# One transposition and one correction product per pair, bias rows per label, and a first pair that mixes time halves as they arrive

## What is computed

```python
x = x + conv_ssm(x masked to t < length[b])       # per channel: causal convolution, kernel of 1024 taps
x = x + einsum('bct,bcd->bdt', x, mix[cond[b]])   # 64x64 matrix of one of 16 conditions, over channels
x = x + x @ W2.T + bias2 + (x @ A2[a[b]].T) @ B2[a[b]].T      # T x T, LoRA of rank 16, 32 adapters
x = x + x @ W3.T + 0.5 * (x @ A3[l[b]]) @ B3.T                # T x T, LoRA of rank 32, 5 labels
```

## Time and profile before

| | |
|---|---|
| median of 3 runs | 1446.25 us (1444.93 to 1446.51) |
| profiled execution, its own time | 1442.18 us |
| span of the core in it | 1440.4 us |
| granted TensorE clock, mean | 1.0 |
| TensorE busy | 1429.8 us, 99% |
| VectorE / ScalarE / GpSimdE busy | 78% / 43% / 7% |
| preparation, convolution, dense part begin at | 0, 177, 549 us |

### The profile page before, as it was taken

The page is one execution under the profiler, slowest core; times in us unless marked ns, Lnnn a source line. Parts: engine busy times, 40 slices in busy tenths (PEclk is TensorE's granted clock), DMA queues, the critical chain, the costliest instruction groups (busy, mean ns, idle before and its releaser), DMA issues.

```text
span 1440.4 us, 31629 instructions
## 1 busy us (share of the span) xinstructions
PE 1429.8 (99%) x9368; PEld 1329.8 (92%) x9368; DVE 1127.4 (78%) x2288; ACT 612.7 (43%) x1217; POOL 100.9 (7%) x193
## 2 busy tenths in 40 slices
PE   9999999999999999999999999999999999999998
PEld 7888899999999999999999999999999999999997
DVE  7975498888888887777777777787777777778775
ACT  4331376666666663333433433433343343343331
POOL 2322100000000002000000000000000000000000
PEclk9999999999999999999999999999999999999999
DMA  8033288888888886564564565556556556555652
GB/s 315 1 129 79 76 283 272 276 277 272 277 268 276 273 274 183 170 203 148 166 200 146 162 197 163 153 182 190 153 162 204 146 161 203 153 153 190 182 154 81
DMA packets 117070, 271.94 MB, mean 189 GB/s; under 512 B 24173, under 2 KB 60401, under 8 KB 114381
## 3 DMA queue, kind: packets, MB, share of 16 engines
q1 hardware_dynamic: 107048, 237.86, 54.1%
q10 hardware_dynamic: 9990, 33.68, 5.8%
HBM read 198.59 MB, written 72.85 MB: 188 GB/s over the span
## 4 chain that ended last, share of the span: by engine, by line
PE 95%; DVE 2%; DMA 2%; SPq 0%; issue 0%; POOL 0%; ACT 0%; DVEq 0%; POOLq 0%; ACTq 0%
PE ps L796 18%; PE ps L789 17%; PE ps L1704 14%; PE ps L788 12%; PE ps L769 8%; PE ps L1603 7%; PE ps L1715 6%; PE ps L805 4%; PE ps L1695 3%; PE ps L1707 2%; PE ps L1589 1%; PE ps L780 1%; PE ps L1612 1%; DMA p<-in_L_cond_base_weight 1%; DMA out<-y_out 1%; PE ps L775 1%
## 5 line engine op out<-in xcount | busy, mean ns | idle before, releaser
L789 PE MATMUL ps<-weights,xa 128*128 128x352 f32 x1152 | 323.0, 322 | 0.0
L788 PE MATMUL ps<-weights,xa 128*128 128x256 f32 x1152 | 321.8, 281 | 0.5 <-ACT y_out L597 0.5
L796 PE MATMUL ps<-weights,xs 128*128 128x512 f32 x1152 | 291.2, 401 | 0.0
L796 PEld LDWEIGHTS ps<-weights,xs 128*128 128x128 f32 x1152 | 207.0, 189 | 40.4
L1704 PE MATMUL ps<-toep,ut 128*128 128x512 f32 (+2 forms) x1152 | 226.7, 342 | 0.0
L788 PEld LDWEIGHTS ps<-weights,xa 128*128 128x128 f32 x1152 | 217.3, 189 | 2.5 <-issue 1.1
L789 PEld LDWEIGHTS ps<-weights,xa 128*128 128x128 f32 x1152 | 216.2, 188 | 1.3
L1704 PEld LDWEIGHTS ps<-toep,ut 128*128 128x128 f32 x1152 | 194.3, 189 | 16.6
L568 ACT ACTIVATE a<-ps 128x512 f32<-128x512 f32 x128 | 76.7, 599 | 281.9 <-PE ps L769 281.2
L769 PE MATMUL ps<-m_gath,x_in 128*128 128x128 f32 x1024 | 134.6, 275 | 1.3 <-DVE x_in L660 1.3
L769 PEld LDWEIGHTS ps<-m_gath,x_in 128*128 128x128 f32 x1024 | 126.6, 191 | 4.0 <-DVE x_in L660 1.5
(11 more groups left out here) (227 smaller groups left out, 2255.3 us busy)
## 6 DMA issues: line engine op xcount, KB each, us to landing
xt<-in_xt SPq DMA_DIRECT2D x64, 512.0 KB, 5.7
x_d<-yo SPq DMA_DIRECT2D x64, 512.0 KB, 2.9
x_nat<-in_x SPq DMA_DIRECT2D x64, 512.0 KB, 3.8
lags<-kern_d SPq DMA_DIRECT2D x63, 512.0 KB, 5.0
x_in<-x_d SPq DMA_DIRECT2D x62, 512.0 KB
out<-y_out ACTq DMA_DIRECT2D x62, 512.0 KB, 5.8
stack<-b_d SPq DMA_DIRECT2D x130, 128.0 KB, 3.9
tab<-a_d SPq DMA_DIRECT2D x128, 128.0 KB, 2.1
```

What stands on the lines that cost most here:

```text
L788: mm(acc[:, left, 0:HALF], x_part, w[:, 0:HALF], start=start, stop=end, skip_group_check=True)
L789: ins = mm(acc[:, right, 0:HALF + KR], x_part, w[:, HALF:WIDE], start=start, stop=end, skip_group_check=True)
L796: ins = mm(acc[:, bank], operand[:, a, i, :], plain(i, b, m), start=opens and i == a == b == 0, stop=i == K4 - 1 and a == 1, skip_group_ch ...
```

## The change

- **Pair, TensorE.** One `hrow`, `hc` and `c_gath` of 128 rows holds both tiles (64 rows each), so one `turn(n)` and one `adapters(n)` serve the pair. `turn` stands in the middle of M6, `adapters` after `quarter(n + 1, 1)`; M4 is no longer cut in two. `low_rank(0, 0, PIECES_S)`, which stood before `quarter(n + 1, 1)`, stands after M3, immediately before `quarter(n + 1, 2)`. Tile 1 has its high rows at 64 and its low rows at 0.
- **Pair, VectorE.** One `h_columns` instead of two, and both `h_stack` after the addition that sets `u2_read`. `first_low(n+1)` comes before `h_columns`.
- **Pair, ScalarE.** No line of it is in the diff.
- **Bias rows.** `row_d` holds a row pair (high and low) for each of the 5 labels. `load_stack` loads two bias rows per batch element, `load_c` no longer loads a bias row. Per pair SyncE issues 12 loads for the stacks (8 before) and 4 for the correction matrix (8 before). `pair_ids` reads four numbers at once; there are four such calls per pair in place of twelve single reads.
- **Preparation.** Bias times A3 moves from job `c` to job `a3b`; job `c` gets five products of one column that turn that row; job `row` gets two more products. `b3n` is loaded and scaled earlier.
- **Start of the dense part.** The last channel's rows go in two halves of time, the front half as soon as it is there. The first pair chooses and mixes three quarters, runs M1, and mixes the fourth after it. The low part of tile 1's table follows the first two choices. `keep_clock` runs 6 products. GpSimdE fills fewer and larger tiles.

```diff
+    b3n, _ = at("b3n", [P, T], F32, o_c - AR // P * 4 * T)
...
-    EVEN_ROWS, LANDED_FIRST = C - 4, 16 * 6
+    EVEN_ROWS, LANDED_FIRST = C - 4, 16 * 4
...
-    FILL_START, FILL_BETWEEN = 20, 12
+    FILL_START, FILL_BETWEEN = 20, 6
...
+    def pair_ids(n, base_of):
+
+        limit = A2N if base_of == B else L3N
+        _, values = nc.values_load_multi_w_load_instructions(index[0:1, bass.ds(4 * n + base_of, 4)], engines=[mybir.EngineType.SP],
+                                                             min_val=0, max_val=limit - 1)
+        return values[0:2], values[2:4]
 
...
+    last_halves = [[sem(f"last_half{h}_{v}") for v in range(2)] for h in range(2)]
+
+    def last_rows(eng, c, v, landed, cols=slice(0, T)):
 
         for b in range(2):
             row = b * C + c
-            eng.dma_start(x1_in[v][row:row + 1], yo[c % 2][2 * v + b:2 * v + b + 1]).then_inc(landed, 16)
-
-    masked = sem("masked")
-
-    def load_stack(eng, v, a):
+            eng.dma_start(x1_in[v][row:row + 1, cols], yo[c % 2][2 * v + b:2 * v + b + 1, cols]).then_inc(landed, 16)
+
+    masked, stack_cleared = sem("masked"), sem("stack_cleared")
+
+    HIGH, LOW = (0, KS), (KS, 0)
+
+    def load_stack(eng, v, a, l):
 
         for b in range(2):
             row = b * (R2 + R3)
-            eng.dma_start(f(stack[v][row:row + R2]), b2_d[bass.ds(a[b], 1)].squeeze(0)).then_inc(stack_landed[v], 16)
-            eng.dma_start(f(stack[v][KS + row:KS + row + R2, 0]),
-                          b2_d[bass.ds(a[b], 1), :, 0, :].squeeze(0)).then_inc(stack_landed[v], 16)
+            high, low, bias = HIGH[v] + row, LOW[v] + row, LOW[v] + 2 * b
+            eng.dma_start(f(stack[v][high:high + R2]), b2_d[bass.ds(a[b], 1)].squeeze(0)).then_inc(stack_landed[v], 16)
+            eng.dma_start(f(stack[v][low:low + R2, 0]), b2_d[bass.ds(a[b], 1), :, 0, :].squeeze(0)).then_inc(stack_landed[v], 16)
+            eng.dma_start(f(stack[v][bias:bias + 2, 1]), row_d[bass.ds(l[b], 1)].squeeze(0)).then_inc(stack_landed[v], 16)
...
-                rows = slice(b * (R2 + R3), b * (R2 + R3) + R2)
-                cols = bass.ds(l[b] * R3, R3)
-                sp.dma_start(c_gath[v][rows, H3], c_adapters[bass.ds(a[b], 1), :, cols].squeeze(0)).then_inc(c_landed[v], 16)
-                sp.dma_start(c_gath[v][KS + b:KS + b + 1, H3], c_d[AR:AR + 1, cols]).then_inc(c_landed[v], 16)
+                row = v * KS + b * (R2 + R3)
+                to = c_gath[row:row + R2, v * KS + R2:v * KS + R2 + R3]
+                sp.dma_start(to, c_adapters[bass.ds(a[b], 1), :, bass.ds(l[b] * R3, R3)].squeeze(0)).then_inc(c_landed[v], 16)
...
+                sp.wait_ge(stack_cleared, 1)
                 for v in range(2):
-                    load_stack(sp, v, first_ids[v])
+                    load_stack(sp, v, first_ids[v], first_ids[2 + v])
                 return
+            a, l = pair_ids(n, B), pair_ids(n, 2 * B)
             sp.wait_ge(p_done, n)
             for v in range(2):
-                load_stack(sp, v, ids(sp, n, v, B))
+                load_stack(sp, v, a[v], l[v])
...
-            a, l = [ids(sp, n + 1, v, B) for v in range(2)], [ids(sp, n + 1, v, 2 * B) for v in range(2)]
+            a, l = pair_ids(n + 1, B), pair_ids(n + 1, 2 * B)
             for v in range(2):
                 sp.wait_ge(h_lo[v], n + 1)
                 load_tables(sp, v, a[v], l[v])
-            sp.wait_ge(adapted, 2 * n + 2)
+            sp.wait_ge(adapted, n + 1)
...
+            pool.wait_ge(last_halves[0][v], 32)
+            pool.wait_ge(last_halves[1][v], 32)
+        nc.gpsimd.tensor_copy(c_gath[:], ident[:]).then_inc(c_fixed, 1)
+        nc.gpsimd.memset(f(stack[1][0:KS, 1]), 0.0).then_inc(stack_cleared, 1)
+        nc.gpsimd.memset(hrow[:], 0.0).then_inc(small_fixed, 1)
+        nc.gpsimd.memset(f(hs[1][0:KS, 1]), 0.0).then_inc(small_fixed, 1)
+        pool.wait_ge(small_fixed, 2)
...
+                nc.gpsimd.tensor_tensor(hs[v][rows, 1, b * C:(b + 1) * C], pair_of[0], pair_of[1], ALU.add).then_inc(small_fixed, 1)
...
-        def h_columns(n, v):
-            dve.wait_ge(turned, 2 * n + v + 1)
-            nc.vector.tensor_copy(hc[v][0:KS], acc[0:KS, SMALL_BANK, 0:P]).then_inc(hc_ready, 1)
+        def h_columns(n):
+            dve.wait_ge(turned, n + 1)
+            nc.vector.tensor_copy(hc[:], acc[:, SMALL_BANK, 0:P]).then_inc(hc_ready, 1)
 
         def h_stack(n, v):
-            low = acc[0:KS, SMALL_BANK, P:2 * P]
-            dve.wait_ge(adapted, 2 * n + v + 1)
-            nc.vector.tensor_copy(hs[v][0:KS], low.unsqueeze(1).to_broadcast([KS, 2, P])).then_inc(hs_hi, 1)
+            high, low = slice(HIGH[v], HIGH[v] + KS), slice(LOW[v], LOW[v] + KS)
+            of = acc[high, SMALL_BANK, P:2 * P]
+            dve.wait_ge(adapted, n + 1)
+            nc.vector.tensor_copy(hs[v][high], of.unsqueeze(1).to_broadcast([KS, 2, P])).then_inc(hs_hi, 1)
             dve.wait_ge(hs_hi, 2 * n + v + 1)
-            tt(hs[v][KS:P, 0], low, f(hs[v][0:KS, 0]), ALU.subtract).then_inc(hs_lo, 1)
-
+            tt(hs[v][low, 0], of, f(hs[v][high, 0]), ALU.subtract).then_inc(hs_lo, 1)
+
+        for v, half in QUARTERS[:2]:
+            choose_first(v, half)
+        h_low(dve, 0, 1)
+        choose_first(*QUARTERS[2])
         first_low(0)
+        choose_first(*QUARTERS[3])
         sums(0)
-        dve.wait_ge(small_fixed, 10)
+        dve.wait_ge(small_fixed, 6)
         dve.wait_ge(x1_stored[1], stored_all)
 
         def pair(n, last_one):
...
             tt(y_out[1][:, HB:T], y_out[0][:, 0:HB], y_out[1][:, HB:T], ALU.add).then_inc(pair_sums, 1)
             dve.wait_ge(m2_done, n + 1)
             h_rows(n, 0)
-            h_columns(n, 0)
             if not last_one:
                 choose(n + 1, 1, 0)
             dve.wait_ge(m4_done, n + 1)
             h_rows(n, 1)
...
-            h_stack(n, 0)
-            h_columns(n, 1)
             if not last_one:
                 first_low(n + 1)
+            h_columns(n)
+            if not last_one:
                 choose(n + 1, 1, 1)
-            h_stack(n, 1)
             dve.wait_ge(m6_done, n + 1)
             dve.wait_ge(pair_sums, 2 * n + 2)
             tt(y_out[0][:, HB:T], y_out[1][:, HB:T], of_p, ALU.add).then_inc(u2_read, 1)
+            for v in range(2):
+                h_stack(n, v)
...
-        def turn(n, v):
-            pe.wait_ge(hrow_ready, 2 * n + v + 1)
-            ready(pe, hs_lo, 2 * n + v)
-            nc.tensor.transpose(acc[:, SMALL_BANK, 0:P], hrow[v][:], ident[:]).then_inc(turned, 1)
-
-        def adapters(n, v):
-            pe.wait_ge(c_landed[v], 64 * n + 64)
-            pe.wait_ge(hc_ready, 2 * n + v + 1)
-            mm(acc[:, SMALL_BANK, P:2 * P], c_gath[v][:], hc[v][:], start=True, stop=True).then_inc(adapted, 1)
+        def turn(n):
+            pe.wait_ge(hrow_ready, 2 * n + 2)
+            ready(pe, hc_ready, n)
+            nc.tensor.transpose(acc[:, SMALL_BANK, 0:P], hrow[:], ident[:]).then_inc(turned, 1)
+
+        def adapters(n):
+            for v in range(2):
+                pe.wait_ge(c_landed[v], 32 * n + 32)
+            pe.wait_ge(hc_ready, n + 1)
+            ready(pe, hs_lo, 2 * n)
+            mm(acc[:, SMALL_BANK, P:2 * P], c_gath[:], hc[:], start=True, stop=True).then_inc(adapted, 1)
...
-        for q in range(4):
+        for q in range(3):
...
+            if isinstance(n, int) and n == 0:
+                quarter(0, 3, FIRST_BANKS[3])
...
-            wide_product(xa22, M4, V_LEFT, V_RIGHT, FRONT, False)
-            turn(n, 0)
-            wide_product(xa22, M4, V_LEFT, V_RIGHT, BACK, False).then_inc(m4_done, 1)
-            adapters(n, 0)
+            wide_product(xa22, M4, V_LEFT, V_RIGHT, ALL, False).then_inc(m4_done, 1)
             if not last_one:
                 quarter(n + 1, 0)
             pe.wait_ge(s2_lo, n + 1)
             ready(pe, y22_added, n)
             plain_product(xs2, M6, P_BANK, FRONT, True)
-            turn(n, 1)
+            turn(n)
             plain_product(xs2, M6, P_BANK, BACK, False).then_inc(m6_done, 1)
-            pe.wait_ge(hs_lo, 2 * n + 1)
-            pe.wait_ge(stack_landed[0], 64 * n + 64)
-            if isinstance(n, int) and n == 0:
-                pe.wait_ge(rows_landed, 16 * 6)
-            low_rank(0, 0, PIECES_S).then_inc(lr11_done, 1)
-            adapters(n, 1)
             if not last_one:
                 quarter(n + 1, 1)
+            adapters(n)
             pe.wait_ge(s4_lo, n + 1)
             ready(pe, y12_added, n)
             plain_product(xs4, M3, Q_BANK, ALL, True)
+            pe.wait_ge(hs_lo, 2 * n + 1)
+            pe.wait_ge(stack_landed[0], 96 * n + 96)
+            if isinstance(n, int) and n == 0:
+                pe.wait_ge(rows_landed, 16 * 4)
+                pe.wait_ge(stack_cleared, 1)
+            low_rank(0, 0, PIECES_S).then_inc(lr11_done, 1)
             if not last_one:
                 quarter(n + 1, 2)
...
+            sp.wait_ge(y_front, C)
```

(57 more changed lines are left out.)

68 lines of the change are left out of this document (25 added, 43 removed).

## The result

| | before | changed kernel |
|---|---|---|
| median | 1445.29 us (6 runs, 1443.25 to 1446.51) | 1536.09 us (6 runs, 1534.74 to 1540.96) |
| profiled execution, span | 1442.18, 1440.4 us | 1537.65, 1535.7 us |
| ratio of times | 1 | 1.0634, 95% interval 1.0617 to 1.0651 |

The changed kernel is 6.3% slower: +90.8 us between the medians, +95.5 between the two profiled executions. The forecast was +55.7 and a range that ended at 1520. The sign and the first mechanism came as forecast; the size did not.

The account below looks back on a forecast made before the run. TensorE, busy 99% of the span, was taken as the bound. Pairs +54.6 us, preparation +2.1, start of the dense part -0.7 and last pair -0.3 gave +55.7 on 1446.25: 1502 us, range 1482 to 1520.

Parts of the forecast that it names:

- Part 1: TensorE in a pair: one adapters and one turn fewer, 0.33 us less, 27.31 us a pair without any new wait.
- Stall one: TensorE before quarter 2 waits for ScalarE's take(n+1, 1), queued behind the low-rank copy: 1.5 us a pair.
- Stall two: TensorE before the pair's last product waits for u3_read, late through ScalarE's table copies and VectorE: about 0.55 us.
- Register reads: SyncE between stack and table issues: a read of four costs like one, saving 5.4 us a pair, worth nothing.
- rival (b): SyncE: a read of four costs four reads, tables land late, u3_read moves by 1.6 us: 1551 us, 7%.
- Preparation: TensorE before the convolution: two more row products and five one-column products, together +2.1 us, from 1.7 to 3.3.
- Start of the dense part: First pair: choosing and M1 start earlier, M2 starts near 558.8, -0.7 us, from -1.2 to +0.5.
- last pair: The final pair, which mixes no successor: -0.3 us.
- Only stall one: Pair: ScalarE and VectorE make up their lateness in M7, so no second stall; 28.8 us a pair, 1484 us, 10%.
- tables late: The same as rival (b): the last table lands after about 23 us in the pair; 1551 us, 7%.
- faster: Before quarter 2: the wait is satisfied when TensorE arrives, only removed work counts; -9.2 us, 1437 us, 2%.
- (c): The same as faster: stall before quarter 2 under 0.33 us; 1437 us, 2%.

Follow-up runs that it names:

- Experiment 2: Changed kernel with ScalarE's take(n+1, 1) and all eight table copies (both h_high) put before the copy that waits for lr11_done: 1442.72 us, ratio 0.9986.
- Experiment 3: Kernel before the change, with only low_rank(0, 0) moved behind M3, just ahead of quarter 2: 1550.99 us, ratio 1.0738.
- Experiment 4: Changed kernel with SyncE's loads of the next x1 held until the pair's last product, so issued with the store: 1509.46 us, ratio 1.0447.
- experiment 1: Changed kernel with only ScalarE's take(n+1, 1) put before the low-rank copy, table copies still behind it: 1494.53 us, ratio 1.0341.
- experiment 5: Kernel of Experiment 2, with VectorE's scaling of b3n moved ahead of b2_low(3): 1438.24 us, ratio 0.9952 to the kernel before the change.
- Experiment 6: Kernel of experiment 5, with the first pair's fourth quarter back ahead of M1: 1437.7 us, ratio 0.9947 to the kernel before the change.

## Why the prediction was wrong in size and right in sign

**Part 1, -0.33 a pair: right.** Experiment 2 leaves no repeated wait and gives 27.37 where 27.31 was forecast.

**Stall one, 1.5 a pair: right.** 1.39 before quarter 2 and 0.12 in it, 1.51. The bracket, 1.26, lies under the forecast's 1.3 by little, because a bracket counts only the idle time; the distance between starts is what a pair pays. Experiment 3 shows it by itself.

**Stall two, 0.55 a pair: right in place, too small.** It measures 0.50 before the last product, and 0.23 behind it, 0.12 of that in the product itself. The failed term is the restart: the forecast put one 0.15 us into the resumption, an estimate that no row showed, and nothing into the products behind it. The last product starts 0.05 us after L755 ends (771.86 + 0.69 = 772.55) but then takes 0.12 longer, and M1's first product 0.10 longer; quarter 2 starts 0.04 after the take ends and takes 0.12 longer. For stall one that comes to the 0.15 assumed, for stall two to more. Against the forecast stall two is short by 0.18 x 31 = 5.6 us.

**M2: the step that failed, put at nothing, +0.91 a pair, 28 us.** The forecast asked "what is late next" along ScalarE and VectorE and stopped at the pair's last product. It should have gone on past the end of the pair: the addition L755 that comes late sets off the others behind it, these the store of the output tile, and the copy L597 of the next pair waits for its landing. The row was there in the kernel before: ScalarE's copy at 752.70 waited 1.64 us for that store, and ended 0.87 us ahead of M2. That was the whole slack, and the copy now comes 1.82 us later, counted from M1 (6.92 against 5.10). Counted from M1 the store is issued as before (0.03 us behind it, before 0.08 ahead). So the lateness of the store alone would have fitted into the slack. But the loads of the next `x1` are released by quarter 3, which stands ahead of stall two; they now go out 0.73 and 0.3 us ahead of M1 where they stood 0.1 ahead and 0.35 behind. Experiment 4 confirms this half (26.6 us back by the order of issue alone), experiments 1 and 3 how it depends on the lead of the loads: 4.6 us for the store where it is issued 1.8 after the first load, 6.9 where 0.65 after. In experiment 1 the loads had moved only 0.18 MB of their 1 MB at the store's issue, and the store had no packet for another 2.0 us; in experiment 3 it had none for 3.0 us. In both it waits until the loads are nearly through. A longer lead only means that they end sooner after its issue.

The Trainium skill, "DMA: Bandwidth & Descriptors", section "Queues, rings and completion order", says that each DMA engine goes round between the queues it has work for, a packet from each. By that rule the store would have had about half of the engines from soon after its issue. The windows of before, 48.7% and 48.0%, agree; those of after show no such sharing, 87.7% for the loads and nothing for a store issued 1.8 us earlier, and experiment 4 shows that a store alone is under way within 1.5 us. The measurement decides: here a store behind two loads of 512 KB waits them out. That need not go against the rule, which speaks only of queues that have work: whether the store's packets stood at the engines in that time or were not made yet, no run here tells.

**Register reads: neither of the two prices.** Between the end of the last stack issue (752.26) and the first table issue (755.70) there are 3.44 us for two calls of four numbers, 1.7 a call, where a single read took 0.68. A call costs like two and a half reads. It is 3.4 us where the forecast wanted under 2, and 2.0 less than before; the tables are not late (rival (b) did not come), as experiment 2 shows.

**Preparation, +2.1, measured +4.1.** The two products, 1.80, and the one-column products, about 0.4, were right. The failed step was a wait put at nothing: the forecast doesn't name the scaling of `b3n` (0.68 us for 32x1024 before, on tile `b3t`, at 110.09 and with no GpSimd instruction beside it), for which `row` now waits. It takes 2.62 here and holds TensorE for 1.90. In experiment 5, without the wait, the convolution starts at 179.08, 2.2 us later than before, where 2.1 was forecast. It ends 0.55 us after GpSimd's `TENSOR_TENSOR` ends (106.37 + 2.62 = 108.99 against 106.10 + 2.34 = 108.44), and in experiment 5, at another place, again 0.55 after (101.75 against 101.20). The Trainium skill, "SBUF — State Buffer", section "SBUF: two separate sides", says that VectorE and GpSimd share one port pair and that the one that comes second is blocked until the other's whole instruction is over. It says so for VectorE's instructions with two SBUF inputs and for those in a two-port mode; this one has one input, and no view tells its mode. The two pairs of rows look like such a block: each ends 0.55 us after GpSimd's instruction, less than the 0.68 it takes by itself.

**Start of the dense part, -0.7, measured +0.44; last pair, -0.3, measured -1.3.** (+0.44 and the forecast are counted to M2.) Choosing began 1.8 us after the convolution's last product had ended, waiting 1.00 us for the front rows; the forecast had them earlier. M1 came 1.8 us earlier relative to the convolution, and M2 gained nothing from it, since the fourth quarter and its copies stood behind M1 (1.13 us bracket). Experiment 6 shows that.

**The sum.** Here the start is counted to M1, so that the pairs begin there. 31 pairs, 92.8 instead of 54.6, are 38.2 of the 39.6 us by which the span's growth (95.3) missed the sum. The first pair, 3.9 us longer, holds what M2 did not gain. The other 1.4 us are the preparation with the first 23 us (5.7 instead of 2.1), the start (-1.8 instead of -0.7) and the last pair (-1.3 instead of -0.3). The medians differ by 4.7 us less than the two profiled executions (95.5), as that of before lay 3.1 under its median and that of after 1.6 above.

**The rivals.** "Only stall one", "tables late" and "faster" did not come. The true case was outside all of them, which is why 1536 lies beyond the range: its bounds came from the sizes of two known stalls, and no part of it stood for a third. The mechanism of (c), the wait satisfied when TensorE gets there, is experiment 2.

## What to carry to other kernels

When a step is moved on one engine, write the order of every engine that waits for it beside it: what is queued there behind the waiting instruction is dragged along, and moving the queue as well can take the loss back (here 93 us). Follow a delay over the end of the loop body, into stores and the buffers that they free, until it meets slack larger than itself. Then ask what did not move with it: where a store has a reader behind it, look at which loads are now issued ahead of it.

## What the runs showed of the hardware that was not expected

- A 512 KB store took at most 3.6 us when issued ahead of 1 MB of loads, 5.2 between them, 6.9 when 0.65 to 0.8 us behind the first of them, and 4.6 when 1.8 us behind it (0.18 MB moved). Behind both loads it had no packet until they were nearly through.
- A one-source VectorE instruction of 32x1024 took 0.68 us alone and 2.62 and 2.63 us when GpSimd's instruction had started 0.27 us before it. The view shows it as running all that time.
- A wait costs TensorE more than its idle bracket. Quarter 2's was 1.26 us and cost the pair 1.51: the start was 1.39 later, and the quarter took 0.92 instead of 0.80, at a granted clock of 1.00.
- In experiment 2 TensorE's granted clock fell to 0.50 for some 3 us after idle stretches of 2.34 and 1.52 us, 1.5 us lost each time; after one of 1.90 us in the changed kernel it did not.
- Reading four numbers into registers in one call took 1.7 us, four single reads 2.7.
